# One group per step, in another order: five engine queues of a graph-attention block reordered, with the output bias made at the first scores

## The reference

```
nx = ln(x)*g1 + b1n;  q, k, v = nx@wq+bq, nx@wk+bk, nx@wv+bv
bias = where(adj > 0, 0.1*adj*adj, -inf)
attn = softmax(q k^T / sqrt(32) + bias);  out = attn v
x1  = x + out@wo + bo
n2  = ln(x1)*g2 + b2n
y   = x1 + gelu(n2@w1 + b1) @ w2 + b2        # 256 -> 1024 -> 256
```

## Time and profile before

| what | value |
| --- | --- |
| median of 3 runs | 1406.34 us (1405.44 to 1407.14) |
| profiled execution: own time, span | 1403.53 us, 1401.6 us |
| mean granted TensorE clock | 0.987 |
| busy: TensorE, VectorE, ScalarE, GpSimd | 97%, 85%, 81%, 40% |
| DMA | 129 GB/s mean |
| chain that ended last | TensorE 91%, ScalarE 5%, VectorE 2% |

### The profile page before, as it was taken

How to read it: one execution, slowest core, us unless ns; L and a number is a source line. 1 busy time by engine, 2 the same in 40 slices (tenths; PEclk the granted TensorE clock), 3 DMA queues, 4 the chain that set the end, 5 groups by cost and what they waited for, 6 DMA issues and landing times.

```text
span 1401.6 us, 34084 instructions
## 1 busy us (share of the span) xinstructions
PE 1357.0 (97%) x11612; PEld 1167.6 (83%) x11612; DVE 1188.8 (85%) x2002; ACT 1135.6 (81%) x3336; POOL 558.4 (40%) x553
## 2 busy tenths in 40 slices
PE   8679999999999999999999999999999999999997
PEld 7568888888888888888888888888888888888876
DVE  4888898888898888898888889888889888889862
ACT  3678889888888888888988888988888888888753
POOL 3353334544333454333545333454333345433320
PEclk8789999999999999999999999999999999999999
DMA  4434333444333444333444433343443344433330
GB/s 150 132 125 143 130 117 122 154 134 144 127 117 125 139 142 142 120 127 121 137 149 131 135 130 118 122 153 127 145 132 110 126 146 142 142 120 121 103 116 23
DMA packets 147257, 180.17 MB, mean 129 GB/s; under 512 B 13584, under 2 KB 130576, under 8 KB 147216
## 3 DMA queue, kind: packets, MB, share of 16 engines
q1 hardware_dynamic: 147216, 179.63, 39.8%
HBM read 95.69 MB, written 83.89 MB: 128 GB/s over the span
## 4 chain that ended last, share of the span: by engine, by line
PE 91%; ACT 5%; DVE 2%; issue 1%; POOL 0%; DMA 0%; SPq 0%; ACTq 0%; DVEq 0%; POOLq 0%
PE work L378 27%; PE work L380 25%; PE work L379 25%; PE area L436 6%; PE work L483 4%; PE work L457 4%; ACT qk_all L656 2%; ACT soft L613 1%; DVE soft L842 0%; ACT late_memory L680 0%; ACT late_memory L691 0%; PE work L385 0%; DMA wa_raw<-in_L_gnn_wq 0%; DVE wa_raw L854 0%; DVE soft L818 0%
## 5 line engine op out<-in xcount | busy, mean ns | idle before, releaser
L613 ACT ACTIVATE soft<-soft,nmax 128x128 f32<-128x128 f32 x1024 | 396.9, 395 | 4.7 <-DVE nmax L826 4.4
L1018 POOL TENSOR_TENSOR ve<-mv,eps 128x4 f32<-128x4 f32 x64 | 13.0, 203 | 771.9 <-DVE mv L891 664.6
L378 PE MATMUL work<-w_hi,hid_parts 128*128 128x256 f32 x1024 | 295.4, 288 | 1.4 <-ACT late_memory L691 1.1
L380 PE MATMUL work<-w_hi,hid_parts 128*128 128x256 f32 x1024 | 286.0, 279 | 0.0
L379 PE MATMUL work<-w_lo,hid_parts 128*128 128x256 f32 x1024 | 285.9, 279 | 0.0
L927 DVE TENSOR_TENSOR hid_parts<-late_memory,hid_parts 128x512 fp32r<-128x512 f32 x256 | 225.2, 882 | 21.8 <-ACT hid_parts L701 21.6
L691 ACT ACTIVATE late_memory<-work,b_col 128x512 f32<-128x512 f32 x256 | 171.9, 683 | 69.6 <-PE work L380 53.3
L378 PE MATMUL work<-nt_hi,w_hi 128*128 128x512 f32 x512 | 211.8, 414 | 3.9 <-DVE nt_lo L917 3.9
L378 PEld LDWEIGHTS work<-w_hi,hid_parts 128*128 128x128 f32 x1024 | 191.9, 187 | 12.0 <-DVE xt_lo L917 5.8
L379 PE MATMUL work<-nt_lo,w_hi 128*128 128x512 f32 x512 | 201.4, 393 | 0.0
L380 PE MATMUL work<-nt_hi,w_lo 128*128 128x512 f32 x512 | 200.5, 392 | 0.0
(11 more groups left out here) (95 smaller groups left out, 3075.7 us busy)
## 6 DMA issues: line engine op xcount, KB each, us to landing
moved_blocks<-wa_raw SPq DMA_DIRECT2D x128, 512.0 KB, 2.7
probt<-moved_blocks SPq DMA_DIRECT2D x512, 128.0 KB, 2.9
xin<-in_x SPq DMA_DIRECT2D x32, 512.0 KB, 3.9
out<-res SPq DMA_DIRECT2D x128, 128.0 KB, 2.1
adj_in<-in_adj SPq DMA_DIRECT2D x32, 256.0 KB, 2.9
res<-in_L_gnn_w SPq DMA_DIRECT2D x1, 1024.0 KB, 9.9
late_memory<-in_L_gnn_w SPq DMA_DIRECT2D x1, 1024.0 KB, 12.4
wa_raw<-in_L_gnn_wq SPq DMA_DIRECT2D x1, 256.0 KB, 3.9
```

The costliest lines, as they stand in the source:

```text
L378: pe.matmul(o, lhs_hi, rhs_hi, start=first, stop=False)
L380: return pe.matmul(o, lhs_lo, rhs_hi, start=False, stop=last)
L613: a = act.activation(soft[:, b % 2, h, :], soft[:, b % 2, h, :], ACT.Exp, bias=nmax[:, b % 2, h:h + 1], accum_out=rsum[:, b % 2, h:h + 1])
```

## The change

Five things are changed.

1. The order of `body` on TensorE, ScalarE, VectorE, GpSimd and SyncE.
2. The table UNITS, and with it the PSUM banks. Transposes nt of a group now stand at the end of the step before that of its `up` (offset -1 instead of -2), all four qk of a group stand in the step before its scores, and down 2 and down 3 stand at the start of the following step (offset -3).
3. `late_rows` is made after the scores of graph 0, not graph 1.
4. `stats1` runs one step earlier and waits for the factors of the group before.
5. EARLY is 6 instead of 4: two more steps are written out ahead of the loop. The adjacency load is issued a step later.

```diff
-UNITS = [("mix", 0, -1, 3), ("nt", 0, -2, 0), ("nt", 1, -2, 1), ("qk", 2, 0, 2), ("qk", 3, 0, 0),
+UNITS = [("down", 2, -3, 0), ("down", 3, -3, 1), ("mix", 0, -1, 3), ("up", 0, -2, 2), ("up", 1, -2, 0),
...
+         ("qk", 1, 1, 2), ("qk", 2, 1, 0), ("qk", 3, 1, 1), ("nt", 0, -1, 2), ("nt", 1, -1, 0)]
-FIRST, EARLY, LATE = -2, 4, 2
+FIRST, EARLY, LATE = -2, 6, 2
...
# SyncE
                 fetch_blocks(step, -1, 1)
                 send_blocks(step, -1, 2)
-                load_adj(step, 2)
+                store(step, -3, 1)
+                store(step, -3, 2)
+                load_adj(step, 1)
+                load_x(step, 2)
                 fetch_blocks(step, -1, 2)
...
# TensorE, score()
-                if b == 1 and step.at_first(off):
+                if b == 0 and step.at_first(off):
                     late_rows()
# TensorE, body, whole new order
+                down(step, -3, 2)
+                down(step, -3, 3)
                 mix(step, -1, 0)
+                up(step, -2, 0)
+                score(step, 0, 0)
+                up(step, -2, 1)
                 project_out(step, -1, 0)
                 up(step, -2, 2)
                 mix(step, -1, 1)
                 up(step, -2, 3)
                 up(step, -2, 4)
+                values(step, 0, 1)
                 project_out(step, -1, 1)
+                score(step, 0, 1)
                 up(step, -2, 5)
+                flip(step, 1, "xt", 0)
+                mix(step, -1, 2)
                 up(step, -2, 6)
+                flip(step, 1, "xt", 1)
                 up(step, -2, 7)
                 project_out(step, -1, 2)
+                values(step, 1, 0)
                 down(step, -2, 0)
+                mix(step, -1, 3)
+                query_key(step, 1, 0)
+                project_out(step, -1, 3)
+                down(step, -2, 1)
+                query_key(step, 1, 1)
+                score(step, 0, 2)
+                query_key(step, 1, 2)
+                query_key(step, 1, 3)
+                flip(step, -1, "nt", 0)
+                flip(step, -1, "nt", 1)
                 score(step, 0, 3)
# ScalarE, around the last hidden slice
                 gelu(step, -2, 7)
+                exponential(step, 0, 0, 0)
                 hidden_hi(step, -2, 7)
# VectorE: maximum() makes late_rows at b == 0; stats1():
+                need(dve, x_rstd, step.through(off - 1, 1, 0))
# VectorE, body: start of the step, and its last lines
+                add_edges(step, -1, 3)
+                flip_lo(step, -2, "nt", 1)
+                maximum(step, -1, 3)
+                invert(step, -1, 2)
+                normalise(step, -1, 2)
+                result(step, -3, 2)
+                result(step, -3, 3)
...
+                turn_blocks(step, 0, 1)
+                flip_lo(step, -1, "nt", 0)
# GpSimd
             def body(step):
-                rstd_of_x(step, 1)
                 result_start(step, -2)
-                rstd_of_n(step, -1)
-                residual_start(step, 0)
+                residual_start(step, 0)
+                rstd_of_x(step, 1)
+                rstd_of_n(step, -1)
                 edges(step, 1)
```

More of the change, by code:

```diff
@@ L342, in body @@
                 fetch_blocks(step, -1, 3)
+                store(step, -3, 3)
+                send_blocks(step, 0, 0)
                 store(step, -2, 0)
[L344 to L345 removed]
                 fetch_blocks(step, 0, 0)
[L347 removed]
                 send_blocks(step, 0, 1)
[L349 to L350 removed]
             steps(sp, groups, body)
@@ L703, in body @@
             def body(step):
-                query_key_copy(step, 0, 1)
+                exponential(step, -1, 2, 0)
+                exponential(step, -1, 2, 1)
+                exponential(step, -1, 3, 0)
                 attn_hi(step, -1, 0)
-                flip_hi(step, -2, "nt", 0)
-                flip_hi(step, -2, "nt", 1)
                 exponential(step, -1, 3, 1)
-                query_key_copy(step, 0, 2)
-                exponential(step, -1, 3, 0)
-                query_key_copy(step, 0, 3)
                 gelu(step, -2, 0)
@@ L742, in body @@
                 query_key_copy(step, 1, 0)
-                exponential(step, 0, 2, 1)
-                exponential(step, 0, 2, 0)
+                query_key_copy(step, 1, 1)
                 norm2(step, -1, 0)
@@ L748, in body @@
                 norm2(step, -1, 3)
-                values_copy(step, 1, 0)
+                query_key_copy(step, 1, 2)
+                query_key_copy(step, 1, 3)
+                flip_hi(step, -1, "nt", 0)
+                flip_hi(step, -1, "nt", 1)
                 if not step.steady and step.n == 0:
@@ L827, in maximum @@
                                   negate=True).then_inc(max_ready, 1)
-                if step.at_first(off) and b == 1:
+                if step.at_first(off) and b == 0:
                     late_rows()
@@ L975, in body @@
                 invert(step, 0, 0)
+                attn_lo(step, -1, 3)
                 normalise(step, 0, 0)
[L977 to L981, removed]
                 residual(step, -1, 3)
@@ L984, in body @@
                 stats2(step, -1)
+                result(step, -2, 0)
+                turn_blocks(step, 0, 0)
                 invert(step, 0, 1)
-                result(step, -2, 2)
+                result(step, -2, 1)
                 normalise(step, 0, 1)
+                add_edges(step, 0, 2)
+                maximum(step, 0, 2)
                 turn_blocks(step, 0, 1)
-                result(step, -2, 3)
-                add_edges(step, 0, 3)
-                maximum(step, 0, 3)
+                flip_lo(step, -1, "nt", 0)
                 if not step.steady and step.n == 0:
@@ L1093, in body @@
             def body(step):
+                result_start(step, -2)
+                residual_start(step, 0)
                 rstd_of_x(step, 1)
-                result_start(step, -2)
                 rstd_of_n(step, -1)
-                residual_start(step, 0)
                 edges(step, 1)
```

73 lines of the change are left out of this document (24 added, 49 removed), and 6 rows, old and new, of the table UNITS.

## The result

The changed kernel takes 1518.75 us (median, 1517.9 to 1522.36) against 1406.44 us: ratio 1.081, 95% interval 1.0796 to 1.0823. It is 112 us slower. 1493 us were forecast, with a range of 1462 to 1530. The span of the profiled execution is 1520.6 us, 119.0 more than before. This execution was the slowest of the four, 3.6 us above the median.

A forecast was written before the change was run, and what follows sets the result against it. TensorE was taken as the bound. Span 1401.6 + 83 (30 steps x 2.75) - 1 (start) - 1.5 (end) + 6 (clock) = 1488, own time 1490, plus 2.8 to the median: 1493 us, range 1462 to 1530.

The forecast's parts named there:

- my main case: Whole kernel: 44.1 to 45.0 us per step, few falls of the clock, 1478 to 1510 us; chance 0.6.
- rival A: Middle steps: the clock falls in most steps, about 1535 us; chance 0.2.
- Down 2 behind the transposes: Each step: down 2 waits for VectorE's remainder of nt 1 to free bank 0; loss 2.3 us, between 2.0 and 3.0.
- Exponential ahead of the last hidden part: Each step, down 0: hidden slice 7 comes late behind table load and exponential; wait 0.55 us, between 0.2 and 1.0.
- What is given back: Each step: the wait for a ScalarE copy in front of the transposes goes, -0.28 us.
- lone units: Each step: more lone short scores, mix or transpose units between products on TensorE, +0.2 to 0.3 us.
- The clock: Middle steps: the new wait lowers TensorE's clock in one step of eight, 4 x 1.6 = +6 us.
- The start: Up to up 0 of group 0: starts at about 92 instead of 93.44 us, -1 us, bounds -10 and +8.
- The end: Last steps: down 2 and 3 of group 30 cover the remainders of nt, -1.5 us, between -4 and +1.
- Rival B: Each step: only the floor of the bank wait, hidden slice 7 in time; step 43.5 us, about 1461 us; chance 0.16.
- rival C: Each step: down 2 does not wait, loss under 0.1 us, about 1401 us, faster or the same; chance 0.04.
- D: Start and middle: the new start saves 10 us but the middle loses 83, 1478 us; no separate chance given.

The follow-up runs named there:

- experiment 1: Changed kernel with only the banks of down 2 and down 3 exchanged: 1426.46 us, ratio 1.0153 to the kernel before.
- number 10: Changed kernel plus 8 identity products between the scores of graph 3 and down 2: 1505.05 us, ratio 1.0710 to the kernel before.
- experiment 9: Kernel before, order kept, other banks: nt 0 takes down 3's, nt 1 qk 1's, units behind follow: 1394.34 us, ratio 0.9921.
- number 3: Changed kernel with banks of down 2 and 3 exchanged and hidden slice 7's main part ahead of the exponential: 1411.81 us, ratio 1.0050.
- experiment 2: Changed kernel with only the main part of hidden slice 7 moved ahead of the exponential: 1495.65 us, ratio 1.0636 to the kernel before.
- number 7: Number 3 with the parts of w1 and w2 made in the middle of step 1, not at the end of step 0: 1409.77 us, ratio 1.0028.
- experiment 5: Kernel before with only the output bias made after the scores of graph 0 instead of graph 1: 1405.31 us, ratio 0.9994.
- Two edits at the start: On number 3: GpSimd's next-group factors ahead of its additions (1411.72 us), w1 and w2 parts in step 1 (1409.77 us); both together 1406.23 us.

## Why the prediction was right

Both waits came where they were forecast, with the causes that were given. The time is 26 us above the 1493, though, and above the band of my main case, 1478 to 1510; it lies in the range because the range took in most of rival A as well. In the profiled execution the sum was 33 us short of the span: 10 from the step, 8 from the clock in the middle, 4 from the start, 12 from the end with the first step that has up. All are errors in the same direction; none made up for another.

*Down 2 behind the transposes, 2.3 us.* Right in place, cause and nearly in size: 2.19 us idle, and a loss of 2.92 - 0.66 = 2.26 us to the next start. Between experiment 1 and the changed kernel the step differs (transposes at 764.99 and 807.23 us in the former) by 44.74 - 42.24 = 2.50 us. The 0.24 us beyond the loss lie behind the wait: the 48 products of down 2 and down 3 take 5.84 us there (726.19 to mix 0) and 5.64 in experiment 1. They take 5.86 in number 10 too, at full clock and without most of the wait, so it is neither the clock nor the idle time. Why they run slower is open.

*Exponential ahead of the last hidden part, 0.55 us.* Right: 0.50 us idle, 42.24 - 41.77 = 0.47 us of step. The copy, the table load and the four exponentials lie as they were summed. The drain that the Trainium skill (ScalarE: Activation LUTs, What ACT_TABLE_LOAD costs) adds is not seen here either: 1.28 us of load at 706.93, and the exponential at 708.23.

*What is given back, and lone units, together -0.1 us.* The sign was wrong: with both waits gone the step is 0.12 us above the old one. The old wait cost 0.36 us, as experiment 9 shows by 41.65 - 41.29, so the new order costs some 0.5 us a step, where I had 0.2 to 0.3. My count was short: on TensorE's timeline of one step, nine runs of short units (transposes, scores, mix) stand between products in number 3 and seven in number 9. I had one more in full and one on the way in. At 0.2 us each, in and out, two more are 0.4 us; that they make the whole is argued, not shown. In the middle, 0.2 us from this term and 0.2 from the slower down 2 and down 3, less 0.1 from the second wait, make 44.74 us a step out of 44.4.

*The clock, +6 us.* Under-sized. I had one step in eight and it was one in three, 14 us. The size of one fall, 1.6 us, was right. Rival A (most steps) did not come. After a wait of 2.13 us the clock had held, and that wait too had a short unit (mix) and the transposes ahead of it; after 2.19 us with transposes and scores ahead of it, it falls in some steps and holds in others. What decides between them is open. The one held clock of the earlier trace rows was too little to set a share of steps by: the one in eight was a guess. The Trainium skill (TensorE: Matmul & The Clock Gate, HAM oscillation — how this bites in real kernels) tells of waits of some 3 to 5 us with a fall behind every one; here the waits are shorter, and it is 9 falls in 28 steps.

*The start, -1 us.* Wrong in sign: up 0 of group 0 starts at 96.12 us, +2.7. Executions with the same order up to there scatter, from 93.93 (experiment 1) to 97.27 us (experiment 2), but all are later than 93.44, the one value that the kernel before has. The first residual began at 32.28 instead of 34.09 us, and it scatters as well (35.26 us in number 7, which differs only later). An earlier bias served nobody, as argued: experiment 5. What I had not seen is that in the new order the bias add of graph 3 stands behind the parts of w1 and w2. TensorE waits for it with the first scores of group 1:

```profile
62.21 1.19 PE L436 MATMUL area<-qk_all 32*128 32x128 f32 x13 [7.25 <-DVE soft L818]
```

*The end, -1.5 us.* Wrong, and the largest error of all. In step 31 the products for a next group are absent, 8 us of TensorE's work. I counted that step shorter by them, as before. But it is 1449.88 - 1403.22 = 46.7 us long, since these products had been the cover of other chains. In number 10 the same stretch takes 45.0 us, with 2.00 us in the last bracket, so 1.7 of the 46.7 are one more fall of the clock:

```profile
1433.62 0.38 PE L378 MATMUL work<-w_hi,hid_parts 128*128 128x256 f32 x1 [1.87 <-DVE hid_parts L928]
1435.83 0.58 PE L378 MATMUL work<-wa_hi,at_hi 128*128 128x256 f32 x1 [1.02 <-DVE at_lo L863]
1445.17 0.73 PE L436 MATMUL area<-qk_all 32*128 32x128 f32 x16 [1.11 <-DVE soft L818]
1449.88 0.58 PE L378 MATMUL work<-w_hi,hid_parts 128*128 128x256 f32 x1 [3.98 <-DVE nt_lo L918]
```

The sum of 119.0 us of span, then: from step 3 to step 31, 1266.7 - 28 x 41.65 = +100.5 us, of which 28 x 2.97 = 83 are the two waits, 14 the clock and 3 the order itself; the start +2.7; the remaining 15.8 the first step with up and the end. The traces of the other experiments divide it. From up 0 of group 0 to down 2 of step 3 the changed kernel takes 40.4 us and number 3 takes 38.0. Behind down 2 of step 31 it takes 117.4 us, number 10 112.7, number 1 104.6 and number 3 103.1. So nearly all of it, some 13 us at the end alone, is again the wait for nt 1's bank and the clock that falls with it; with both waits cured nothing of it is left. I had priced the last steps like the others, and took off 1.5 us for a cover by down 2 and down 3 that themselves wait for that bank.

Rival B was excluded by the bias add, which began at T + 2.02 behind the first remainder, while the scores had ended at T + 1.70, and by the second wait, rival C by the wait itself, and D had no gain at the start to offer.

## What to carry to other kernels

When a list of units is reordered on an engine that is nearly always busy, follow for each unit the last user of its buffer, and what the releasing engine has queued in front of the release. A wait that a step has at all, it has in every step: 2.2 us became 92 us here, with the clock and the end of the run, and exchanging two bank numbers took them away. Look at the remaining waits of the old kernel in the same manner: its own 0.28 us per step was a bank as well, and worth 11 us.

## What the runs showed that was not expected

- With waits of 2.19 us, each step alike, the clock fell in 9 steps of 28 and held in the others; with the same waits, but without the one of 0.50 us elsewhere in the step (experiment 2), it fell in 3 of 28. Each is one profiled execution. The mean clocks of the unprofiled ones point the same way: 0.970 for the changed kernel, 0.974 to 0.978 for experiment 2. Filling the same wait with idle products held it at 1.00 in the middle and was worth 13.7 us, though down 2 came no sooner behind the scores.
- A wait of 0.28 us, taken away, gave 0.36 us of step. Taking away the 2.19 us gave 2.50. In both cases the idle time in brackets is less than what the step gains; the distance between starts (0.36 and 2.26 us) is nearer.
- Two edits at the start that gave 0 and 2 us one by one gave 5.6 us together; by the ratios it is 0, 3 and 6.
